# A two-layer cross-attention kernel on one core: second-layer token-major projections in pairs of 64-column tiles in place of quarters of 32

## What is computed

```
# layer 0
h = layernorm(x) * gamma + beta
Q, K, V = h @ Wq, ctx @ Wk, ctx @ Wv              # 16 heads of 64
x = x + (softmax(Q K^T) * scale @ V) @ Wo + bo
# layer 1
xn = x * rsqrt(mean(x*x) + eps) * norm_w
q, k, v = xn @ wq, ctx @ wkv[:, :512], ctx @ wkv[:, 512:]   # 16 heads of 32
q, k = rotate(q), rotate(k); q, k = q/|q|, k/|k|
x = x + (softmax(sqrt(32) q k^T) @ v) @ wout
```

## Time and profile before

| | us |
|---|---|
| median of 3 runs | 3315.94 |
| lowest and highest of them | 3315.68, 3317.42 |
| the profiled execution | 3319.18 |
| its span, first to last instruction | 3317.4 |
| PE busy in the span | 3093.1 (93%) |
| PEld busy | 1565.2 (47%) |
| DVE busy | 2385.6 (72%) |
| ACT busy | 1409.6 (42%) |

### The profile page before, as it was taken

The page is one execution under the profiler, slowest core; times in us unless marked ns, Lnnn a source line. Parts: engine busy times, 40 slices in busy tenths (PEclk is TensorE's granted clock), DMA queues, the critical chain, the costliest instruction groups (busy, mean ns, idle before and its releaser), DMA issues.

```text
span 3317.4 us, 73642 instructions
## 1 busy us (share of the span) xinstructions
PE 3093.1 (93%) x31708; PEld 1565.2 (47%) x31708; DVE 2385.6 (72%) x2804; ACT 1409.6 (42%) x1728; POOL 499.0 (15%) x221
## 2 busy tenths in 40 slices
PE   5999999899999999988999999998999999999897
PEld 3555555444355555544345555454434455555441
DVE  3677776787777776678777777668876767766877
ACT  2333333456433333355643333345563333334565
POOL 1000002343000000335100000033410000013440
PEclk8999999999999999999999999999999999999999
DMA  3001010201111010011111110101112010100001
GB/s 109 19 21 25 21 25 16 58 24 37 45 50 28 21 25 21 22 54 24 36 48 49 25 25 21 25 19 56 28 33 72 22 27 21 25 21 22 19 16 36
DMA packets 178409, 107.32 MB, mean 32 GB/s; under 512 B 81452, under 2 KB 147116, under 8 KB 178088
## 3 DMA queue, kind: packets, MB, share of 16 engines
q1 hardware_dynamic: 178088, 102.60, 11.7%
HBM read 93.12 MB, written 9.42 MB: 31 GB/s over the span
## 4 chain that ended last, share of the span: by engine, by line
PE 82%; DVE 9%; issue 4%; ACT 3%; DMA 1%; SPq 1%; DVEq 0%; POOL 0%; ACTq 0%; POOLq 0%
PE o_acc L663 19%; PE scores L651 19%; PE work L691 13%; PE work L686 11%; PE work L713 9%; PE work L619 5%; DVE acc L810 4%; PE work L706 2%; ACT probs L740 2%; PE work L696 2%; DVE tile_max L791 1%; DVE resid L895 1%; DVE stats L830 1%; PE work L701 1%; PE work L723 1%
## 5 line engine op out<-in xcount | busy, mean ns | idle before, releaser
L740 ACT ACTIVATE probs<-scores 128x1024 f32<-128x1024 f32 x1024 | 996.4, 1023 | 481.6 <-PE scores L651 472.2
L810 DVE TENSOR_TENSOR acc<-acc,probs 128x1024 f32<-128x1024 f32 x768 | 983.8, 1304 | 21.4 <-DVE acc L810 1.8
L791 DVE TENSOR_REDUCE tile_max<-work 128x2 f32<-128x1024 f32 x496 | 607.2, 1224 | 523.5 <-PE work L619 519.9
L663 PE MATMUL o_acc<-probs,v_tok 128*64 128x512 f32 (+1 forms) x4096 | 778.5, 611 | 0.3 <-ACT probs L740 0.3
L925 POOL TENSOR_TENSOR inv<-sumsq,power 128x16 f32<-128x16 f32 x64 | 231.2, 3613 | 2066.7 <-DVE sumsq L876 2066.6
L713 PE MATMUL work<-wo,o_sum 128*32 128x512 f32 (+1 forms) x2072 | 401.5, 602 | 41.7 <-issue 28.4
L651 PE MATMUL scores<-q_high,k_high 32*128 32x512 f16 (+1 forms) x2048 | 309.1, 392 | 77.1 <-ACT probs L740 55.9
L663 PEld LDWEIGHTS o_acc<-probs,v_tok 128*64 128x64 f32 (+1 forms) x4096 | 165.6, 122 | 349.7 <-issue 334.5
L651 PE MATMUL scores<-q_high,k_low 32*128 32x512 f16 (+1 forms) x2048 | 303.6, 384 | 0.0
L651 PE MATMUL scores<-q_low,k_high 32*128 32x512 f16 (+1 forms) x2048 | 303.0, 383 | 0.0
L895 DVE TENSOR_TENSOR resid<-work,resid 128x512 f32<-128x512 f32 x384 | 261.8, 685 | 45.3 <-PE work L713 44.9
(11 more groups left out here) (76 smaller groups left out, 2660.3 us busy)
## 6 DMA issues: line engine op xcount, KB each, us to landing
recip<-rows_dram SPq DMA_DIRECT2D x380, 64.0 KB, 2.2
stage<-in_x_dram SPq DMA_DIRECT2D x8, 1024.0 KB, 6.6
wq<-in_L_xattn_Wq_dram SPq DMA_DIRECT2D x32, 256.0 KB, 2.7
resid<-in_x_dram SPq DMA_DIRECT2D x8, 1024.0 KB, 5.3
wo<-in_L_xattn_Wo_dram SPq DMA_DIRECT2D x32, 256.0 KB, 2.7
out_dram<-resid SPq DMA_DIRECT2D x8, 1024.0 KB, 4.4
wk<-in_L_xattn_Wk_dram SPq DMA_DIRECT2D x32, 192.0 KB, 2.4
wv<-in_L_xattn_Wv_dram SPq DMA_DIRECT2D x32, 192.0 KB, 2.5
```

Source lines behind the costliest of these rows:

```text
L663: mm = pe.matmul(o_acc[h * d:(h + 1) * d, :], v_tok[par][:, kt, h * d:(h + 1) * d], probs[:, unit_slot(t, n, kt, h // 2), h % 2, :], start ...
L740: act.activation(probs[:, no % RING, :, :], scores[:, unit_banks(t, n, kt, u), :], ACT.Exp, scale=(1.0, float(D1) ** 0.5 / QK_SCALE ** 2)[ ...
L791: dve.tensor_reduce(tile_max[:, qt, :, n:n + 1], maxima_banks(e), AX.X, ALU.max, negate=True).then_inc(dve_freed, 1)
L810: dve.tensor_tensor(a[:, heads, :], before, probs[:, unit_slot(t, n, kt, u), :, :], ALU.add).then_inc(add_ok, 1)
```

## The change

In `number`, entries of the kinds `v`, `kr` and `qr` get `e.cols = D0`, that is 64, wherever they stand in a turn's step; the others keep the width of the turn of their step. Only entries in steps of layer 1 change by this, since 64 is what they had in steps of layer 0. The same products are summed in the same banks; no other engine's instructions differ.

```diff
             items[e.kind, e.t, e.i] = e
             if st.t is not None:
-                e.cols = WIDTH_OF[st.t]
+                e.cols = D0 if e.kind in ("v", "kr", "qr") else WIDTH_OF[st.t]
             if e.kind not in WORK:
```

## The result

| | before | changed |
|---|---|---|
| median of 8 runs, us | 3315.81 | 3324.97 |
| lowest and highest | 3312.1, 3317.42 | 3321.91, 3329.82 |
| the profiled execution | 3319.18 | 3324.63 |
| its span | 3317.4 | 3322.8 |

The medians lie 9.2 us apart. The ratio is 1.0033, with a 95% interval from 1.0022 to 1.0043: 7 to 14 us slower, where 11.0 were forecast.

The account below looks back on a forecast made before the run. PE was taken to bound the kernel, busy for 93% of the span. Switches and slow starts add 12.0 us, less 1.05 swallowed, so 11.0 us on the median 3315.94: 3326.9 us, 0.33% slower, range 3320 to 3332.

Parts of the forecast that it names:

- Groups cost the same in either width, and a switch 0.12 us: In projections, a column-tile group takes 0.218 us at 32 or 64 columns; each change of form costs PE 0.12 us.
- The price per record: Rival: each matmul record costs time, so 4000 fewer in layer 1 gain; 3307 us at 5 ns each; chance 0.05.
- The sign that I gave for the stretches: In the changed kernel's trace, layer 1's four stretches each 2 to 3.5 us longer, layer 0 not at all.
- PE-bound wherever a step holds a projection: In layer 1, steps with a projection are paced by PE, so delays there reach the end.
- What is swallowed: Delays of PE hidden beside other waiting: 1.05 us of the 12.0 us, leaving 11.0 us.
- The last `kr` of t11: Three of four are followed by a wait of PE for DVE, which swallows 0.15 us each: -0.45 us.
- The two `v` of t11: In batch 0 their delay of 0.30 us goes under in a wait, once.
- the two projections ahead of the first `out` of t8: In batch 0 their 0.30 us goes under, as DVE waits for a DMA; elsewhere the wait passes a delay on.
- the sum: Over layer 1's 74 changed entries, switches and slow starts add 12.0 us on PE, 11.0 after what is swallowed.

Follow-up runs that it names:

- e1: Changed kernel with only the last of four token tiles of each changed entry in 64 columns; 1.0040 against the kernel before, medians 12.6 us apart.
- e2: Changed kernel with token tiles of each changed entry alternating between 64 and 32 columns; 1.0108 against the kernel before, medians 35.1 us apart.
- e5: Kernel before with layer 0's values, rotated keys and queries also in 32 columns; 1.0025 against the kernel before, medians 8.4 us apart.
- e8: The changed kernel unedited, run once more; 1.0030 against the kernel before (1.0019 to 1.0041).
- e10: The kernel before unedited, as a kernel of its own; 0.9999 against the kernel before, medians 0.3 us apart.
- e6: Changed kernel with layer 1's output projections also in 64 columns; 1.0031 against the kernel before, medians 11.3 us apart.
- e9: Kernel before with only layer 1's out entries that are alone in their step in 64 columns; 1.0005, medians 1.2 us apart.
- e11: Kernel before with the next batch's loads issued four steps later, behind the denominators' round trip; 0.9993, medians 2.3 us apart.
- e4: Changed kernel with the changed entries in one tile of 128 columns; 1.0041 against the kernel before, medians 13.5 us apart.
- e3: Kernel before with only layer 1's values in 64 columns, keys and queries in 32; 1.0021, medians 6.1 us apart.
- e7: Kernel before with only layer 1's rotated keys and queries in 64 columns, values in 32; 1.0022, medians 7.1 us apart.

## Why the prediction was right, and where not

**Groups cost the same in either width, and a switch 0.12 us: right.** The entries of the trace above are within 0.02 us of the forecast prices. e1 and e2 show that it is the switch that is paid, e5 that it is paid in the other direction too. The price per record, the rival on the other side, falls with the entries: from its start to the scores behind it a `v` takes 2.74 us with 96 records, 2.77 with 48 and 2.88 with 24. The sign that I gave for the stretches, each 2 to 3.5 us longer, was too narrow: they were 1.6 to 4.4 us longer in the first trace, and e8's are 1.5 to 5.4 us longer than e10's. One execution scatters by more than that, in part by its clock.

**PE-bound wherever a step holds a projection: right, and the step on which most hung.** e6 and e9 show that without it the count of switches forecasts nothing. When I set the expectation of e6 I forgot my own condition.

**What is swallowed: right in kind, too small in size.** The last `kr` of t11 behaved as forecast: from its start to the start of the `den` it is 3.97 us in both kernels in batches 0 to 2, the longer inside taken out of the wait. The kernel before, whose `den` is in the earlier trace rows, and the changed one:

```profile
745.89 2.83 PE L691 MATMUL work<-wk,cT 128*32 128x128 f32 x96
```

```profile
744.19 2.84 PE L691 MATMUL work<-wk,cT 128*64 128x128 f32 x48
...
748.16 1.06 PE L706 MATMUL work<-acc,ones_plain 128*32 128x512 f32 x8 [1.13 <-DVE resid L895]
```

The two `v` of t11 behaved as forecast as well. Their 0.30 us passed on in batches 1 to 3 (15.3 us from the `den` to the first `out` of that half before, 15.6 after), and in batch 0, where PE waited 1.02 us, they went under.

But I let the two projections ahead of the first `out` of t8 go under in batch 0 alone, since DVE's idle time there ended with a DMA only in batch 0. Their 0.30 us doesn't show in batches 1 and 2 either. From the `den` to that `out` the kernel before took 19.69, 19.64, 19.57 and 18.44 us, and e8 19.62, 20.08, 19.62 and 18.57 us. The first trace of the changed kernel has 21.12, 19.62, 19.62 and 20.22 us, with some 1.6 us of the slow clock in the first and the last. In it DVE waited 0.15, 0.19 and 0.79 us for the reciprocals ahead of the normalization (L819) in batches 0 to 2. Where it waits, the normalization starts 3.3 to 3.7 us after SP has issued the read of the reciprocals. In batch 1 of the kernel before it started 4.2 us after that (4.9 in e10), without a wait, directly behind the rotation of a `kr` that a stall had made late (below). So there the reciprocals took the place of the late `kr`, and the `out` started no later. In batch 2 it was 3.5 us, and either may have set it. In batch 3, which has neither, 0.13 of the 0.30 us reached the `out`.

Why the reciprocals are so late stands in SP's timeline of the kernel before, batch 1: the loads of `stage` and `c_ring` are issued between the read of the sums and the write of the reciprocals (L549), whose landing SP waits for until 1470:

```profile
1458.97 0.37 SPq L543 DMA_DIRECT2D den_t<-rows_dram  x1
1459.39 1.06 SPq L519 DMA_DIRECT2D stage<-in_x_dram  x2
1460.49 1.22 SPq L527 DMA_DIRECT2D c_ring<-in_ctx_dram  x2
1461.75 0.68 SPq L549 DMA_DIRECT2D rows_dram<-recip_t  x1
1470.14 1.72 SPq L554 DMA_DIRECT2D recip<-rows_dram  x4
```

From the write to the read of the reciprocals it is 8.7, 8.4 and 9.0 us in batches 0 to 2. With the loads behind the round trip, in e11, it is 2.6, 3.2 and 2.5 us, here in batch 0:

```profile
644.81 0.37 SPq L549 DMA_DIRECT2D rows_dram<-recip_t  x1
647.38 1.92 SPq L554 DMA_DIRECT2D recip<-rows_dram  x4
...
649.81 1.06 SPq L519 DMA_DIRECT2D stage<-in_x_dram  x2
```

That is another 0.6 us that did not arrive: with it the sum would have been 12.0 - 1.65 = 10.3 us, nearer to the measured 9 to 11. If 1.6 us of those are the clock's, as estimated above, somewhat more went under than this names, and where is open. e2 and e4 came out at 0.88 and 0.73 of their PE time, so longer delays meet still more cover.

**A gain that I had not seen, and that goes under at the same place.** In batches 0 to 2 the kernel before stalls beside those loads. In batch 1 it is in the middle of a run of scores, then `kr`, attend and the wait for the `out`:

```profile
1465.73 0.38 PE L651 MATMUL scores<-q_low,k_low 32*128 32x512 f16 x3
1467.49 0.38 PE L651 MATMUL scores<-q_low,k_low 32*128 32x512 f16 x1 [1.38 <-issue]
1467.81 1.06 PE L663 MATMUL o_acc<-probs,v_tok 128*32 128x512 f32 x8
1468.69 2.80 PE L691 MATMUL work<-wk,cT 128*32 128x128 f32 x96
...
1475.10 1.07 PE L713 MATMUL work<-wo,o_sum 128*32 128x512 f32 x8 [1.64 <-issue]
```

In the changed kernel the stall is gone, and the wait has grown from 1.64 to 3.07 us:

```profile
1465.34 1.06 PE L663 MATMUL o_acc<-probs,v_tok 128*32 128x512 f32 x8
1466.33 2.84 PE L691 MATMUL work<-wk,cT 128*64 128x128 f32 x48
...
1474.22 1.06 PE L713 MATMUL work<-wo,o_sum 128*32 128x512 f32 x8 [3.07 <-issue]
```

The stalls of the kernel before are 0.5, 1.8 and 0.9 us in batches 0 to 2, and 0.6, 2.1 and 0.6 in e10. All six traces with 32-column `kr` and the loads at this place (before, e3, e5, e9, e10 and, with its last tile in pairs, e1) have such a stall in at least two batches, none of the traces with halved, quartered or alternating `kr` (changed, e2, e4, e6, e7, e8) has one. The removed stalls, some 3 us of PE time, bring next to nothing in the changed kernel, since DVE waits for the reciprocals ahead of the `out` behind them. Where it doesn't, they arrive in part: in batch 1 of e6 and e7 that `out` starts 18.57 us after its `den`.

What PE lacked in these stalls is, by the traces, instructions. The page lists a DMA queue of the kind `instruction`, first before and then in the changed kernel (packets, MB, share of the engines):

```profile
q8 instruction: 255, 4.18, 0.6%
q8 instruction: 223, 3.65, 0.5%
```

With fewer instructions on PE it has fewer packets, of 16 KB each. In batch 1 of the kernel before, one began at 1448.63 and the next only at 1465.13, with the loads between them; it took 0.88 us, and PE went on at 1467.49, 1.48 us after its end. At every such stall of the six traces PE went on 1.2 to 1.5 us after the end of a packet of this queue, and the kernel before and e10 stalled at the same records of the same operations. No run changes the supply alone, so this is read from the times. That the loads delay these packets rests on the time at which the stalls come and on e11, which has none; how they do it is open.

## What to carry to other kernels

Price an array's tile width by its neighbours, not by its matmul count: tiles of one form run on, with their weights loaded ahead, and each change of form costs a fixed 0.11 to 0.15 us here. Then ask of each switch what its step waits for; beside a wait for another engine it was free as far as could be measured (42 switches, 1.2 us), in steps paced by the matmul engine nearly all of it arrived (37 switches, 6.1 us). And look at the wait behind a stall before counting on the stall's removal.

## What the runs showed of the hardware that I had not expected

- Twelve groups of one 128-column matmul (e4, 2.88 us to the scores) are slower than of two 64-column ones (2.77) or, with the weights loaded ahead, four 32-column ones (2.74): the fewest instructions were the slowest. Most of that is the first matmul behind the change of form, 0.213 us in place of 0.112.
- PE stalled for 0.2 to 3.3 us inside or beside 32-column projections while 2.4 MB of loads had just been issued, each time until 1.2 to 1.5 us after a packet of the instruction queue was in, and in no trace where the keys' entries were halved.
- The small write of the reciprocals, behind which SP could go on after 2.5 to 3.2 us in e11, held it for 8.4 to 9.0 us when those loads had been issued just ahead (in batch 1 1461.75 to 1470.14).
